# Order of scores, bias, and input parts in a fused attention and layer norm kernel

## The chip, the core and the metric

The kernel runs on one core of a Trainium2 chip. The metric is the time of one launch on the device, in microseconds (us), the median of several runs. The core has a matmul engine (PE, with its weight loads shown as PEld), three engines for elementwise work, DVE, ACT and GpSimd (POOL in the profile), and SP, which here issues the DMAs. The engines run side by side and wait for one another on semaphores. Matmul results land in PSUM, everything else lies in SBUF.

## What is computed

128 graphs of 128 nodes with 384 features, 12 heads of 32:

```python
q = (x @ Wq.T).reshape(B, N, 12, 32)
k = (x @ Wk.T).reshape(B, N, 12, 32)
v = (x @ Wv.T + bv).reshape(B, N, 12, 32)
a = einsum('bnhd,bmhd->bhnm', q, k) * SCALE + adj[:, None]
pad_mask = all(a == 0, axis=-1)
a = nan_to_num(softmax(where(pad_mask[..., None], -inf, a)))
o = einsum('bhnm,bmhd->bnhd', a, v).reshape(B, N, 384)
out = layernorm(x + o @ Wo.T + bo)
```

## The kernel before

The kernel works on graphs one by one, and on inputs by quads of four graphs; there are 32 quads. In a quad q the four stretches are called G0 to G3 here, one per graph. Every engine has its own program, written by hand in a fixed order, and `over_quads` unrolls it; each program runs ahead or behind by a fixed number of graphs.

For accuracy, the operands of the projections are split in two parts, `hi` and `lo`, and `split_product` (L208) adds three products in one PSUM bank. ACT makes `xT_hi` from `xT_raw` (`keep_xT_hi`, L375), DVE subtracts to make `xT_lo` (`keep_xT_lo`, L484), in three parts of 128 features per quad. `xT_raw` is a single buffer, loaded by SP (`load_xT`).

PE per stretch b, before: attention of graph b (`attend`, L252: twelve products, each on 32 columns of the array), the scores of graph b + 2 (`scores`, L229: twelve products, each on 32 rows of the array), six transposes of the probabilities of graph b + 1 (`transpose_probs`, L240), a projection of v or of q and k for a later graph or quad (L211 to L213), the output projection of graph b (`project_out`, L265), six more transposes, and one or two more projections. At the end of G2 stands `project_qk` of part 0 for the quad after next, which waits for all three parts of its `xT_lo` (`pe.wait_ge(xT_lo_done, CHUNKS * q + 3 * CHUNKS)`, L323).

DVE per stretch b (`graph`, L578): `keep_oT_lo` (after ACT's `oT_hi`), four bias trios for graph b + 2 (`bias_trio`, L504, adds the bias to three heads and finds the row maximum), in some stretches `keep_xT_lo` or `keep_v`, the first half of the mask (`mask_half`: `neg_sum`, `inv_sum`, `live`, `row_scale`), the residual (`y_sb`), `stats`, `mean_var`, `var_eps`, then `normalise` (`out_sb`), which waits for GpSimd's `inv_std`, and the second half of the mask.

ACT per stretch (L413): `oT_hi`, two copies of transposed probabilities to `pT` (L401), exponentials of graph b + 2 in trios, two more copies to `pT`, the last exponentials, with the copies `qkT` and `xT_hi` between them.

GpSimd per stretch (L664): `fold_half` twice, `scale_half` (multiplies the probabilities by `row_scale`), `inverse_std`, `add_bo` (adds the output bias to x of the next graph, in SBUF), `scale_half` for the other half.

Of the kernel before, what the change touches and what calls it, by code (L numbers as in the profile page):

```python
# [26 lines left out]
CHUNKS = HIDDEN // P  # L27
ROWS = P // HEAD
QUAD = 4
QUADS = BATCH // QUAD  # L30
# [15 lines left out]
def attention_kernel(nc, x, xT, adj, wq_t, wk_t, wv_t, wo_t, bv, bo, out):  # L46
# [7 lines left out]
    with ctx:  # L54
# [100 lines left out]
        def _(sp):  # L155
# [27 lines left out]
            load_x(QUAD, 1)  # L183

            def quad(j, p, has_next, has_after):
                q = 2 * j + p

                if has_after:
                    sp.wait_ge(xT_lo_done, CHUNKS * q + 2 * CHUNKS)
                    load_xT(q + 2)  # L190
                for b in range(QUAD):
                    sp.wait_ge(out_done, QUAD * q + b + 1)
                    sp.dma_start(out[bass.ds(QUAD * q + b, 1), :, :].rearrange("b n f -> n (b f)"),
                                 out_sb[:, b, :]).then_inc(out_stored[b], 16)
                    if b == 1 and has_after:
                        sp.wait_ge(neg_a_done, 16 * q + 16)
                        load_adj(QUAD * q + 2 * QUAD, p)
                if has_after:
                    load_x(QUAD * q + 2 * QUAD, p)
# [7 lines left out]
        def _(pe):  # L207
# [65 lines left out]
            def quad(j, p, has_next, has_after):  # L273
                q = 2 * j + p
                nxt, aft = ahead(j, p, 1), ahead(j, p, 2)

                pe.wait_ge(y_read, QUAD * q + 1)
                attend(j, p, 0)
                pe.wait_ge(neg_a_done, 16 * q + 8)
                scores(j, p, 2)  # L280
# [9 lines left out]
                if has_next:  # L290
                    pe.wait_ge(y_read, QUAD * q + 2)
                    project_qk(*nxt, 3, 0)
                pe.wait_ge(v_done, QUAD * q + 4)
                attend(j, p, 1)
                pe.wait_ge(neg_a_done, 16 * q + 12)
                scores(j, p, 3)
# [11 lines left out]
                attend(j, p, 2)  # L308
                if has_next:
                    pe.wait_ge(qk_done, QK * q + 2 * QK)  # L310
                    pe.wait_ge(neg_a_done, 16 * q + 16)
                    scores(*nxt, 0)
                transpose_probs(j, p, 3, 0)
# [12 lines left out]
                if has_next:  # L326
                    pe.wait_ge(v_done, QUAD * q + QUAD + 2)
                attend(j, p, 3)
                if has_next:
                    pe.wait_ge(neg_a_done, 16 * q + 20)  # L330
                    scores(*nxt, 1)
                    transpose_probs(*nxt, 0, 0)
# [41 lines left out]
        def _(act):  # L374
# [38 lines left out]
            def graph(j, p, b, has_next, has_after):  # L413
# [19 lines left out]
                if b == 2 and has_after:  # L433
                    keep_xT_hi(*aft, 2)
# [7 lines left out]
                if b == 0 and has_after:  # L442
                    act.wait_ge(v_psum, QUAD * (2 * j + p) + QUAD)
                    keep_xT_hi(*aft, 0)
                if b == 1 and has_next:
                    keep_qk(*nxt, 5, turn)
                if b == 3 and has_after:
                    keep_qk(*aft, 2, turn)
                if b == 1 and has_after:
                    keep_xT_hi(*aft, 1)  # L450
# [32 lines left out]
        def _(dve):  # L483
# [94 lines left out]
            def graph(j, p, b, has_next, has_after):  # L578
                nxt, aft = ahead(j, p, 1), ahead(j, p, 2)
                turn = 1 - ATTEND_BANK[b]  # L580
                more2 = b + 2 < QUAD or has_next
                keep_oT_lo(j, p, b)
                if more2:
                    for trio in range(4):
                        bias_trio(*later(j, p, b, 2), trio)
# [9 lines left out]
                statistics(j, p, b)  # L595
                mean_variance(j, p, b)
                add_eps(j, p, b)
                if b == 2 and has_after:
                    keep_xT_lo(*aft, 1)
                    keep_xT_lo(*aft, 2)  # L600
# [34 lines left out]
        def _(pool):  # L635
# [28 lines left out]
            def graph(j, p, b, has_next):  # L664
                more2 = b + 2 < QUAD or has_next
                if more2:
                    fold_half(*later(j, p, b, 2), 0)
                    fold_half(*later(j, p, b, 2), 1)
                    scale_half(*later(j, p, b, 2), 0)
                inverse_std(j, p, b)  # L670
                if b + 1 < QUAD or has_next:
                    add_bo(*later(j, p, b, 1))
# [53 lines left out]
```

## Time and profile before

| | |
|---|---|
| median of 3 runs | 1276.09 us (1274.07 to 1276.71) |
| profiled execution | 1274.01 us, span 1272.2 us |
| busy: PE, PEld | 1225.0 us (96%), 1053.9 us (83%) |
| busy: DVE, ACT, POOL | 1039.1 us (82%), 1022.4 us (80%), 859.3 us (68%) |
| granted clock of PE | 0.995 of full speed |
| DMA | 70 GB/s on average |

Busy shares are of the span. A busy PE isn't PE at its peak, since matmuls overlap. The quads repeat: each takes 38.87 us. So one of them, from 619.78 us to 658.65 us, is read below in order of time. A timeline row gives the start in us from the start of the span, the duration in us, the engine, the line, the operation, what it writes and what it reads, how many were merged, and in brackets the idle time ahead of it and who ended that.

### The profile page before, as it was taken

The page shows a single profiled execution, that of the slowest core. Times are in us where ns is not written, and L with a number is a line of the kernel's source. Part 1 is how long each engine was busy: PE and PEld are TensorE (multiplying, and loading weights), DVE is VectorE, ACT ScalarE, POOL GpSimd, SP SyncE. Part 2 cuts the span into 40 slices and gives each one's busy share as a digit, 9 for nine tenths or more (in the row PEclk, how much of TensorE's full clock was granted, in tenths as well). Part 3 has the DMA queues.
Part 4 walks back from the last instruction along what each step waited for, and adds up shares of the span by engine and source line. Part 5 has one row for each costly group of instructions (what it writes and reads, how often), then busy time and mean ns, then how long its engine had stood idle before and what let it go on. Part 6 is the DMA issues. An engine that isn't in the chain of part 4 may idle for free.

```text
span 1272.2 us, 34265 instructions
## 1 busy us (share of the span) xinstructions
PE 1225.0 (96%) x11742; PEld 1053.9 (83%) x11742; DVE 1039.1 (82%) x5094; ACT 1022.4 (80%) x4007; POOL 859.3 (68%) x775
## 2 busy tenths in 40 slices
PE   8999999999999999999999999999999999999986
PEld 7888888888888888888888888888888888888875
DVE  5778888888888788888888887888888888878886
ACT  6877888878788778888887887788887878877874
POOL 1766767667667667676676676676766766766675
PEclk9999999999999999999999999999999999999998
DMA  6022112222122221122221222211222202222100
GB/s 228 22 70 84 61 46 84 78 70 78 34 79 78 70 84 59 47 84 78 70 78 34 79 78 70 84 63 43 84 78 70 78 32 80 79 70 84 47 26 32
DMA packets 58895, 88.85 MB, mean 70 GB/s; under 512 B 3680, under 2 KB 54624, under 8 KB 58720
## 3 DMA queue, kind: packets, MB, share of 16 engines
q1 hardware_dynamic: 58720, 86.65, 20.2%
q8 instruction: 93, 1.52, 0.5%
q14 instruction: 82, 0.67, 0.2%
HBM read 61.47 MB, written 25.17 MB: 68 GB/s over the span
## 4 chain that ended last, share of the span: by engine, by line
PE 70%; DVE 24%; issue 3%; POOL 2%; ACT 1%; DMA 0%; DVEq 0%; POOLq 0%; SPq 0%
PE turn_bank L211 16%; PE turn_bank L213 16%; PE turn_bank L212 16%; PE pT_bank L248 9%; PE score_bank L235 7%; PE turn_bank L260 6%; DVE neg_a L511 6%; DVE out_sb L575 3%; DVE xT_lo L487 3%; DVE stats L560 3%; DVE y_sb L555 3%; DVE neg_sum L523 2%; POOL inv_std L661 1%; DVE v_sb L501 1%; DVE mean_var L564 1%
## 5 line engine op out<-in xcount | busy, mean ns | idle before, releaser
L396 ACT ACTIVATE probs<-neg_a,neg_max 128x128 f32<-128x128 f32 x1536 | 596.6, 398 | 1.9 <-DVE neg_max L511 1.9
L654 POOL TENSOR_TENSOR probs<-probs,row_scale 128x768 f32<-128x768 f32 x256 | 376.6, 1471 | 191.7 <-DVE row_scale L539 191.7
L647 POOL TENSOR_TENSOR fold<-neg_a 128x384 f32<-128x384 f32 x256 | 271.8, 1062 | 168.6 <-DVE neg_max L511 168.6
L511 DVE CUSTOM_DVE_ANT_0 neg_a<-score_bank,adj_sb 128x128 f32<-128x128 f32 x1536 | 333.2, 285 | 0.2
L403 ACT ACTIVATE pT<-pT_bank 128x384 f32<-128x384 f32 x512 | 220.8, 485 | 103.4 <-PE pT_bank L248 103.3
L396 ACT ACTIVATION_READ_ACCUMULATOR probs<-neg_a,neg_max 128x1 f32 x1536 | 302.8, 197 | 0.0
L211 PE MATMUL turn_bank<-xT_hi,w_hi 128*128 128x512 f32 x576 | 241.0, 418 | 29.4 <-DVE xT_lo L487 27.6
L213 PE MATMUL turn_bank<-xT_hi,w_lo 128*128 128x512 f32 x576 | 227.7, 395 | 0.0
L212 PE MATMUL turn_bank<-xT_lo,w_hi 128*128 128x512 f32 x576 | 227.6, 395 | 0.0
L248 PE MATMUL pT_bank<-ident,probs 128*128 128x128 f32 x1536 | 217.3, 278 | 0.3 <-ACT pT L403 0.3
L389 ACT ACTIVATE qkT<-turn_bank 128x512 f32<-128x512 f32 x192 | 113.7, 592 | 100.2 <-PE turn_bank L213 96.8
L248 PEld LDWEIGHTS pT_bank<-ident,probs 128*128 128x128 f32 x1536 | 173.9, 141 | 20.9 <-issue 1.2
L575 DVE TENSOR_SCALAR out_sb<-y_sb,mean_var,inv_std 128x384 f32<-128x384 f32 x128 | 124.1, 969 | 43.3 <-POOL inv_std L661 43.3
L211 PEld LDWEIGHTS turn_bank<-xT_hi,w_hi 128*128 128x128 f32 x576 | 108.5, 188 | 57.3 <-DVE xT_lo L487 39.2
L548 DVE TENSOR_TENSOR oT_lo<-turn_bank,oT_hi 128x384 fp32r<-128x384 f32 x128 | 71.1, 555 | 93.2 <-ACT oT_hi L409 93.2
L640 POOL TENSOR_TENSOR x_sb<-x_sb,bo_sb 128x384 f32<-128x384 f32 x128 | 131.9, 1030 | 19.5 <-DMA x_sb<-x_dram 19.5
L523 DVE TENSOR_REDUCE neg_sum<-fold 128x6 f32<-128x384 f32 x256 | 138.8, 542 | 2.6 <-POOL fold L647 2.6
L211 PE MATMUL turn_bank<-w_hi,xT_hi 128*128 128x384 f32 x384 | 140.0, 365 | 0.0
L211 PE MATMUL turn_bank<-w_hi,oT_hi 128*128 128x384 f32 x384 | 130.0, 339 | 1.9 <-DVE oT_lo L548 1.7
L213 PE MATMUL turn_bank<-w_hi,oT_lo 128*128 128x384 f32 x384 | 129.9, 338 | 0.0
L212 PE MATMUL turn_bank<-w_lo,oT_hi 128*128 128x384 f32 x384 | 129.8, 338 | 0.0
L213 PEld LDWEIGHTS turn_bank<-xT_hi,w_lo 128*128 128x128 f32 x576 | 108.1, 188 | 26.1
(38 smaller groups left out, 2021.9 us busy)
## 6 DMA issues: line engine op xcount, KB each, us to landing
xT_raw<-xT_dram SPq DMA_DIRECT2D x32, 768.0 KB, 6.3
x_sb<-x_dram SPq DMA_DIRECT2D x32, 768.0 KB, 5.2
out_dram<-out_sb SPq DMA_DIRECT2D x128, 192.0 KB, 1.9
adj_sb<-adj_dram SPq DMA_DIRECT2D x32, 256.0 KB, 3.0
w_raw<-wq_t_dram SPq DMA_DIRECT2D x1, 576.0 KB, 5.7
w_raw<-wk_t_dram SPq DMA_DIRECT2D x1, 576.0 KB, 6.8
w_raw<-wv_t_dram SPq DMA_DIRECT2D x1, 576.0 KB, 7.8
w_raw<-wo_t_dram SPq DMA_DIRECT2D x1, 576.0 KB, 8.4
```

The lines of the kernel that those rows point to most:

```text
L211: nc.tensor.matmul(dst, stat_hi(c), mov_hi(c), start=(c == 0), stop=False)
L212: nc.tensor.matmul(dst, stat_hi(c), mov_lo(c), start=False, stop=False)
L213: last = nc.tensor.matmul(dst, stat_lo(c), mov_hi(c), start=False, stop=(c == CHUNKS - 1))
L248: last = nc.tensor.transpose(pT_bank[r][:, c * N:(c + 1) * N], probs[b % 2][:, 3 * trio + c, :], ident[:, :])
L396: last = nc.scalar.activation(probs[b % 2][:, u, :], neg_a[b % 2][:, u, :], ACT.Exp, bias=neg_max[b % 2][:, u:u + 1], scale=-1.0, accum_ou ...
L403: nc.scalar.activation(pT[:, CHUNKS * trio:CHUNKS * (trio + 1), :], pT_bank[trio % 2][:, 0:HIDDEN].rearrange("p (c n) -> p c n", c=CHUNKS) ...
L511: last = nc.vector.tensor_tensor_reduce(out=neg_a[b % 2][:, u, :], in0=score_bank[trio][:, c * N:(c + 1) * N], in1=adj_sb[p][:, b, :], sca ...
L523: nc.vector.tensor_reduce(neg_sum[:, u], fold[:, u, :], AX.X, ALU.add).then_inc(mask_steps, 1)
L575: nc.vector.tensor_scalar(out_sb[:, b, :], y_sb[:, :], mean_var[:, 0:1], inv_std[:, 0:1], ALU.subtract, ALU.mult).then_inc(out_done, 1)
L640: nc.gpsimd.tensor_tensor(x_sb[p][:, b, :], x_sb[p][:, b, :], bo_sb[:, :], ALU.add)\
L647: nc.gpsimd.tensor_tensor(fold[:, u, :], neg_a[b % 2][:, u, 0:N // 2], neg_a[b % 2][:, u, N // 2:N], ALU.add).then_inc(fold_done, 1)
L654: nc.gpsimd.tensor_tensor(probs[b % 2][:, u, :], probs[b % 2][:, u, :], row_scale[:, u].unsqueeze(2).broadcast_to([P, HALF, N]), ALU.mult) ...
```

## The change

No operation is added or taken away. On PE, the scores go ahead of the attention in G0, G1 and G3, and behind the first transposes in G2. On DVE, the first bias trio goes ahead of `keep_oT_lo` in G0, G1 and G3; part 1 of `xT_lo` moves from G2 to G1, and part 2 stands ahead of `mean_variance` in G2. On ACT, `xT_hi` parts 0 and 1 are made in G0, part 2 in G1. On GpSimd, `add_bo` goes ahead of the first `scale_half`. On SP, `xT_raw` is loaded three quads ahead, in G3, and no longer two quads ahead at the start of the quad.

```diff
@@ sync
+            sp.wait_ge(xT_lo_done, 2 * CHUNKS)
+            load_xT(2)
...
-                if has_after:
-                    sp.wait_ge(xT_lo_done, CHUNKS * q + 2 * CHUNKS)
-                    load_xT(q + 2)
                 for b in range(QUAD):
+                    if b == 3 and q + 3 < QUADS:
+                        sp.wait_ge(xT_lo_done, CHUNKS * q + 3 * CHUNKS)
+                        load_xT(q + 3)
@@ tensor
+                pe.wait_ge(neg_a_done, 16 * q + 8)
+                scores(j, p, 2)
                 pe.wait_ge(y_read, QUAD * q + 1)
                 attend(j, p, 0)
-                pe.wait_ge(neg_a_done, 16 * q + 8)
-                scores(j, p, 2)
...
+                pe.wait_ge(neg_a_done, 16 * q + 12)
+                scores(j, p, 3)
                 pe.wait_ge(v_done, QUAD * q + 4)
                 attend(j, p, 1)
-                pe.wait_ge(neg_a_done, 16 * q + 12)
-                scores(j, p, 3)
...
                 attend(j, p, 2)
+                transpose_probs(j, p, 3, 0)
                 if has_next:
                     pe.wait_ge(qk_done, QK * q + 2 * QK)
                     pe.wait_ge(neg_a_done, 16 * q + 16)
                     scores(*nxt, 0)
-                transpose_probs(j, p, 3, 0)
...
                 if has_next:
+                    pe.wait_ge(neg_a_done, 16 * q + 20)
+                    scores(*nxt, 1)
                     pe.wait_ge(v_done, QUAD * q + QUAD + 2)
                 attend(j, p, 3)
                 if has_next:
-                    pe.wait_ge(neg_a_done, 16 * q + 20)
-                    scores(*nxt, 1)
@@ scalar
-                if b == 2 and has_after:
+                if b == 1 and has_after:
                     keep_xT_hi(*aft, 2)
...
                     keep_xT_hi(*aft, 0)
+                    keep_xT_hi(*aft, 1)
...
-                if b == 1 and has_after:
-                    keep_xT_hi(*aft, 1)
@@ vector
+                if b != 2 and more2:
+                    bias_trio(*later(j, p, b, 2), 0)
                 keep_oT_lo(j, p, b)
                 if more2:
-                    for trio in range(4):
+                    for trio in range(0 if b == 2 else 1, 4):
                         bias_trio(*later(j, p, b, 2), trio)
...
                 statistics(j, p, b)
+                if b == 2 and has_after:
+                    keep_xT_lo(*aft, 2)
                 mean_variance(j, p, b)
                 add_eps(j, p, b)
-                if b == 2 and has_after:
+                if b == 1 and has_after:
                     keep_xT_lo(*aft, 1)
-                    keep_xT_lo(*aft, 2)
@@ gpsimd
                     fold_half(*later(j, p, b, 2), 1)
+                if b + 1 < QUAD or has_next:
+                    add_bo(*later(j, p, b, 1))
+                if more2:
                     scale_half(*later(j, p, b, 2), 0)
                 inverse_std(j, p, b)
-                if b + 1 < QUAD or has_next:
-                    add_bo(*later(j, p, b, 1))
                 if more2:
                     scale_half(*later(j, p, b, 2), 1)
```

Three places in the order of instructions. The lines of the changed kernel stand two to four further down. First, PE at the start of G2: the attention of graph 2 (the row that writes `turn_bank` from `pT`), the scores of the next quad's graph 0, the transposes of graph 3, and the first projection of v. Before:

```order
L260 MATMUL turn_bank<-pT,v_sb 32x128 x12
L235 MATMUL score_bank<-qkT 128x128 x12
L248 MATMUL pT_bank<-ident,probs 128x128 x6
L211 MATMUL turn_bank<-w_hi,xT_hi 128x384
L212 MATMUL turn_bank<-w_lo,xT_hi 128x384
```

Changed:

```order
L262 MATMUL turn_bank<-pT,v_sb 32x128 x12
L250 MATMUL pT_bank<-ident,probs 128x128 x6
L237 MATMUL score_bank<-qkT 128x128 x12
L213 MATMUL turn_bank<-w_hi,xT_hi 128x384
L214 MATMUL turn_bank<-w_lo,xT_hi 128x384
```

The scores now stand behind the six transposes.

Second, DVE in G2, from behind the bias and `v_sb`: the mask's first half, the residual, the statistics and the parts of `xT_lo`. Before:

```order
L523 TENSOR_REDUCE neg_sum<-fold 128x6
L528 RECIPROCAL inv_sum<-row_sum 128x6
L533 TENSOR_TENSOR live<-neg_max,neg_sum 128x6
L539 TENSOR_TENSOR row_scale<-live,inv_sum 128x6
L555 TENSOR_TENSOR y_sb<-turn_bank,x_sb 128x384
L560 BN_STATS stats<-y_sb 128x6
L564 BN_AGGR mean_var<-stats 128x2
L568 TENSOR_SCALAR var_eps<-mean_var 128x1
L487 TENSOR_TENSOR xT_lo<-xT_raw,xT_hi 128x512 x2
L501 TENSOR_TENSOR v_sb<-turn_bank,bv_sb 128x384
```

Changed:

```order
L524 TENSOR_REDUCE neg_sum<-fold 128x6
L529 RECIPROCAL inv_sum<-row_sum 128x6
L534 TENSOR_TENSOR live<-neg_max,neg_sum 128x6
L540 TENSOR_TENSOR row_scale<-live,inv_sum 128x6
L556 TENSOR_TENSOR y_sb<-turn_bank,x_sb 128x384
L561 BN_STATS stats<-y_sb 128x6
L488 TENSOR_TENSOR xT_lo<-xT_raw,xT_hi 128x512
L565 BN_AGGR mean_var<-stats 128x2
L569 TENSOR_SCALAR var_eps<-mean_var 128x1
L502 TENSOR_TENSOR v_sb<-turn_bank,bv_sb 128x384
```

One part of `xT_lo` is left in G2, and it stands two places earlier.

Third, GpSimd in any stretch of the steady part, from the two folds on. Before:

```order
L647 TENSOR_TENSOR fold<-neg_a 128x384 x2
L654 TENSOR_TENSOR probs<-probs,row_scale 128x768
L661 TENSOR_TENSOR inv_std<-var_eps,minus_half 128x1
L640 TENSOR_TENSOR x_sb<-x_sb,bo_sb 128x384
L654 TENSOR_TENSOR probs<-probs,row_scale 128x768
```

Changed:

```order
L651 TENSOR_TENSOR fold<-neg_a 128x384 x2
L644 TENSOR_TENSOR x_sb<-x_sb,bo_sb 128x384
L658 TENSOR_TENSOR probs<-probs,row_scale 128x768
L665 TENSOR_TENSOR inv_std<-var_eps,minus_half 128x1
L658 TENSOR_TENSOR probs<-probs,row_scale 128x768
```

`add_bo` (the row that writes `x_sb`) moved from behind `inv_std` to behind the folds.

## Rows read from the trace of the kernel before

**Rows 1.** Waits of PE: for whom, us in total, times, longest

```profile
PE turn_bank L211 <- DVE xT_lo L487: 27.6, 30, 1.1
PE turn_bank L260 <- ACT pT L403: 6.9, 4, 2.7
```

**Rows 2.** Timeline of PE, one steady quad: start, duration, line

```profile
627.35 0.34 PE L213 MATMUL turn_bank<-w_hi,xT_lo 128*128 128x384 f32 x1
...
629.39 0.40 PE L213 MATMUL turn_bank<-xT_hi,w_lo 128*128 128x512 f32 x1
629.72 0.86 PE L260 MATMUL turn_bank<-pT,v_sb 128*32 128x128 f32 x24
...
638.66 0.86 PE L260 MATMUL turn_bank<-pT,v_sb 128*32 128x128 f32 x24
639.45 0.95 PE L235 MATMUL score_bank<-qkT 32*128 32x128 f32 x24
640.33 0.88 PE L248 MATMUL pT_bank<-ident,probs 128*128 128x128 f32 x6
640.96 0.42 PE L211 MATMUL turn_bank<-w_hi,xT_hi 128*128 128x384 f32 x1
...
647.47 0.50 PE L211 MATMUL turn_bank<-xT_hi,w_hi 128*128 128x512 f32 x1 [0.91 <-DVE xT_lo L487]
```

**Rows 3.** Timeline of DVE, the same quad, and its last `out_sb`

```profile
627.72 0.56 DVE L501 TENSOR_TENSOR v_sb<-turn_bank,bv_sb 128x384 f32<-128x384 f32 x1 [0.49 <-PE turn_bank L213]
...
634.17 0.69 DVE L487 TENSOR_TENSOR xT_lo<-xT_raw,xT_hi 128x512 fp32r<-128x512 f32 x1
...
635.36 0.40 DVE L533 TENSOR_TENSOR live<-neg_max,neg_sum 128x6 f32<-128x6 f32 x1
...
638.29 1.15 DVE L575 TENSOR_SCALAR out_sb<-y_sb,mean_var,inv_std 128x384 f32<-128x384 f32 x1 [0.67 <-POOL inv_std L661]
...
640.29 0.56 DVE L548 TENSOR_TENSOR oT_lo<-turn_bank,oT_hi 128x384 fp32r<-128x384 f32 x1
640.77 0.28 DVE L511 CUSTOM_DVE_ANT_0 neg_a<-score_bank,adj_sb 128x128 f32<-128x128 f32 x1
...
643.30 0.55 DVE L501 TENSOR_TENSOR v_sb<-turn_bank,bv_sb 128x384 f32<-128x384 f32 x1
...
644.35 0.17 DVE L533 TENSOR_TENSOR live<-neg_max,neg_sum 128x6 f32<-128x6 f32 x1
644.55 0.17 DVE L539 TENSOR_TENSOR row_scale<-live,inv_sum 128x6 f32<-128x6 f32 x1
644.63 0.55 DVE L555 TENSOR_TENSOR y_sb<-turn_bank,x_sb 128x384 f32<-128x384 f32 x1
645.22 0.56 DVE L560 BATCH_NORM_STATS2 stats<-y_sb 128x6 f32<-128x384 f32 x1
...
646.10 1.31 DVE L487 TENSOR_TENSOR xT_lo<-xT_raw,xT_hi 128x512 fp32r<-128x512 f32 x2
...
1269.35 0.48 DVE L575 TENSOR_SCALAR out_sb<-y_sb,mean_var,inv_std 128x384 f32<-128x384 f32 x1 [0.66 <-POOL inv_std L661]
```

**Rows 4.** Timeline of GpSimd (POOL), the same quad

```profile
634.34 1.40 POOL L647 TENSOR_TENSOR fold<-neg_a 128x384 f32<-128x384 f32 x1 [0.25 <-DVE neg_max L511]
...
638.22 1.00 POOL L640 TENSOR_TENSOR x_sb<-x_sb,bo_sb 128x384 f32<-128x384 f32 x1
...
643.46 1.03 POOL L647 TENSOR_TENSOR fold<-neg_a 128x384 f32<-128x384 f32 x1 [0.25 <-DVE neg_max L511]
644.79 1.47 POOL L654 TENSOR_TENSOR probs<-probs,row_scale 128x768 f32<-128x768 f32 x1 [0.30 <-DVE row_scale L539]
646.26 0.95 POOL L661 TENSOR_TENSOR inv_std<-var_eps,minus_half 128x1 f32<-128x1 f32 x1
```

**Rows 5.** Timeline of ACT, the `pT` pair ahead of attention 2

```profile
636.68 0.86 ACT L403 ACTIVATE pT<-pT_bank 128x384 f32<-128x384 f32 x2
```

## The prediction

> **What bounds the kernel now.** I read the waits first, then one steady quad in order of time, engine by engine. The waits of the matmul engine [rows 1] show it almost never idle: 27.6 us before L211, released by DVE's `xT_lo` (L487), 30 times, and 6.9 us in 4 waits for `pT`, which lie at the first and the last graphs. In the steady quad from 619.78 to 658.65 us the only stop of PE is the one at 647.47 [rows 2]: `project_qk` of the quad after next needs all three `xT_lo` parts, and DVE ends the last two at 646.10 + 1.31 = 647.41 [rows 3]; PE goes 0.06 later. Call the four stretches of a quad G0 to G3, each from one attention to the next: attention 1 stands at 629.72 (A1), attention 2 at 638.66 (A2) [rows 2]. That projection starts 8.81 after A2 (647.47 - 638.66). So PE's length is settled in G2 by a chain on DVE: first bias 640.77, last bias ends 643.30, `y_sb` 644.63, `stats` 645.22, `xT_lo` pair 646.10 [rows 3].
>
> **How DVE and GpSimd meet.** This decides the case. `live` (L533), a DVE operation with two SBUF inputs, takes 0.17 at 644.35. At 635.36 it takes 0.40: it ends at 635.76, 0.02 after the `fold` that GpSimd runs from 634.34 to 635.74 [rows 3, 4]. That `fold` is itself stretched to 1.40 from the 1.03 of the one at 643.46: it began 0.17 after an `xT_lo` on DVE that ends at 634.86 [rows 3, 4], and from there runs 0.88, so 0.15 of its start-up was done while it stood. `out_sb` (L575) takes 1.15 at 638.29, beside `add_bo` (638.22, 1.00), and 0.48 at 1269.35 with GpSimd idle [rows 3, 4]. And `inv_std` at 646.26, where the `xT_lo` pair was already queued, takes 0.95, ending well behind the first of them. So of the two, the one that comes second stands until the first has ended. The Trainium skill, "SBUF — State Buffer", section "Who interferes with whom", has the same rule: a DVE instruction with two SBUF inputs contends with a GpSimd instruction that reads SBUF, and whichever issues first keeps the pair while the other fully blocks. The rows agree (0.40, 1.15, 1.40); it speaks against this change.
>
> **The change, part by part.**
> (1) Scores ahead of attention in G0, G1, G3. PE does the same work. Each switch between full-array, row-tiled and column-tiled matmuls leaves 0.33 between starts (629.39 to 629.72) where the spacing is 0.23, so 0.10 a switch [rows 2]. Before: projection, attention, scores, transposes, three switches; now three too. I take 0; the new pairs may cost or return 0.05 each, so up to 0.15 in three stretches, 4 us either way in all. In G2 the order is now attention, transposes, scores, projection. Transposes run from 640.33 to the projection at 640.96, 0.63, and there was no switch behind them [rows 2]; now there is one ahead of the scores and one behind: scores start at A2 + 0.79 + 0.80 = 1.59, and PE's own work up to the projection grows by 0.2. If PE set the end that were 6 us over 30 quads; beside the chain below it is hidden. The Trainium skill, "TensorEngine Tiling (Array Packing)", section "Key Properties", says that changing the tiling mode drains TensorE; the 0.33 agrees, and by that rule alone the change costs those 6 us.
> (2) One trio of the bias (three of 0.21, 0.63) ahead of `oT_lo` in G0, G1, G3. DVE waits there for `oT_hi` anyway, and the scores now come 0.88 earlier (the length of scores, 639.45 to 640.33 [rows 2]). So in G1 the last bias ends 0.63 earlier: it ended at 634.17, A1 + 4.45 [rows 3]; now A1 + 3.82. `oT_lo` isn't later.
> (3) The copies `xT_hi` on ACT. Part 2 moves from G2 into G1, ahead of `pT` for attention 2. The pair of `pT` starts at 636.68, A1 + 6.96, and takes 0.86 [rows 5]. Now transposes come 0.88 earlier after A1 and the copy (no longer than the 0.69 of its DVE twin) is added: end about 7.63, while A2 comes at 8.94 - 0.88 = 8.06. Hidden, 0.4 to spare; were the cover gone it would cost at most 0.3 a quad. Part 1 goes behind `exp` of G0, where nothing waits for it. The load of `xT` is issued a graph before the old place: SP is past its wait for `out_done` there, and the stores and the `adj` and `x` loads keep their order. Nothing.
> (4) `xT_lo` part 1 goes to G1, behind `var_eps`; part 2 stands alone in G2, ahead of `mean_var`. By DVE's own times that is the gain: from first bias to `y_sb` 3.86, to `stats` 0.59, then 0.48 (as from `oT_lo` 640.29 to the bias 640.77) to `xT_lo`, 0.69, 0.06 to PE [rows 3].
> (5) `add_bo` now stands between the second `fold` and the first `scale`. Before, GpSimd was idle there, and after `inv_std` it ran beside `out_sb`. Now `add_bo` starts as `fold` ends. `row_scale` has two SBUF inputs and comes after that: in G2 `fold` ends at 643.46 + 1.03 = 644.49, `row_scale` starts 644.55 [rows 3, 4]. It stands for the whole of `add_bo`, and with it all that is queued on DVE (`y_sb`, `stats`, `xT_lo`, `out_sb`). In return `out_sb` runs beside an idle GpSimd, 0.48 instead of 1.15.
>
> **The walk.** G1, from the last bias E1 = A1 + 3.82: `xT_lo` part 0 starts, `fold` ends E1 + 1.57 (as 635.74 - 634.17), `add_bo` + 2.57, `row_scale` ends + 2.59, `y_sb` starts 0.09 before that (644.72, 644.63), + 2.50. `xT_lo` part 1 is issued 1.47 later (646.10 - 644.63), + 3.97. `scale` starts 0.07 after `row_scale` ends, + 2.66, and takes 1.47, + 4.13; `xT_lo` ends 0.55 after that, `inv_std` + 5.08. From `out_sb` to the next `oT_lo` it was 2.00 (638.29 to 640.29); less 0.67, 1.33: `oT_lo` at + 6.43, which is A1 + 10.25 = A2 + 2.19. It was A2 + 1.63. First bias 0.48 later, A2 + 2.67 [rows 3, 4]. The scores would allow 2.57: last column group 0.67 after the start at 1.59, and 0.31 until DVE sees it (L501 came 0.37 after the start of the last matmul at 627.35, of which 0.06 is its greater width [rows 2, 3]).
> G2: last bias ends 2.67 + 2.53 = 5.20; `fold` 5.36 to 6.39; `row_scale` would come at 2.67 + 3.78 = 6.45, 0.06 too late; `add_bo` until 7.39, `row_scale` ends 7.41, `y_sb` 7.32, `stats` 7.91, `xT_lo` issued 8.39. `scale` runs from 7.48 to 8.95, so `xT_lo` ends at 9.50 and PE goes at 9.56, against 8.81: 0.75 longer. G0 and G3 lose time on DVE as well. From a last bias: `fold` ends 1.19, `add_bo` 2.19, `scale` 2.3 to 3.75, `inv_std` at most 0.67 more (the wait at 638.29), 4.4, next bias trio 1.33 later, 5.75, then 0.63, `oT_lo` 0.48, nine biases 1.90: 8.8 for a round. Those stretches last 8.9 to 9.9 without a wait, so PE isn't held there; the margin in the short one is 0.1. PE itself would be ready at 7.94.
> 30 quads x 0.75 = +22.5 us. Ends: the scores now fill part of the waits for `pT` at the start and the end, about 0.9 in each of four: -3.5. 1274.0 + 19.0 = 1293.0; the median of the runs is 2.1 above the profiled one, so 1295.
>
> **Rivals.**
> A, faster: GpSimd and DVE don't hold each other up in the new places (`scale` has been seen ahead of `xT_lo` only with its last 0.16, at 646.10). Then bias at 2.57, `y_sb` 6.43, `stats` 7.02, `xT_lo` 7.50 to 8.19, PE 8.25: 0.56 less a quad, 16.8, with the ends 20.3: 1256. It decides whether `xT_lo` of G2 gets in ahead of `scale`: unheld it comes at 7.50, while `scale` behind `add_bo` comes at 7.3, a margin of 0.2. For it: that margin is small. Against: the 0.40 of `live`, an operation of the same kind, in the same place.
> B, halfway: `row_scale` is held and `scale` doesn't hold `xT_lo`: 8.39 + 0.69 + 0.06 = 9.14, + 0.33, so +9.9 - 3.5: 1282.5.
> C, the gain of (4) and the loss of (5) cancel, for instance if `add_bo` slips behind `row_scale` and `xT_lo` is held for half of `scale`: 8.8, no change but the ends, about 1273.
> If only `scale` holds, and not `add_bo`, the end is 7.39 + 1.47 + 0.55 + 0.06 = 9.47, and the forecast stands.
>
> **How the numbers follow.** Forecast 0.64, A 0.17, B 0.14, C 0.05. Unknowns of the forecast: switches of PE 4 us either way, the ends 2, the walk 0.1 a quad, 3. The likeliest case alone reaches from 1288 to 1301. The range goes down over B and C to 1267 and leaves A out. Within 0.2% is about what a measurement of this kernel can't tell from none. Faster 0.19, same 0.04, slower 0.77.
>
> **What would show it.** In the profile after: `row_scale` (L539 before) near 1.0 instead of 0.17 where `add_bo` runs; `out_sb` near 0.5 on average; `xT_lo` of G2 well over 0.69, ending with `scale` + 0.55; PE's wait for `xT_lo` still there, 30 times, about 1.6 each; the quad 39.6 instead of 38.87. Wrong, if `row_scale` stays at 0.17 and that wait shrinks to about 0.3: then A.

## The result and the profile after

The changed kernel takes 1297.6 us (median of 4 runs, 1297.0 to 1298.2), the kernel before 1275.1 (median of 4 runs beside it, 1274.1 to 1276.7): a ratio of 1.0175, 95% interval 1.0158 to 1.0193. It is slower by 1.75%, as forecast (1295.0, range 1267 to 1301). The profiled execution took 1297.29 us, its span 1295.5, the granted clock 0.996 of full speed.

The waits of PE, total, times and longest, in the kernel after. The first row answers to [rows 1], where it was 27.6 us:

```profile
PE turn_bank L213 <- DVE xT_lo L488: 43.4, 30, 1.5
PE turn_bank L213 <- DVE oT_lo L549: 5.3, 6, 1.2
PE turn_bank L262 <- DVE y_sb L556: 3.0, 2, 1.9
```

The three groups of DVE instructions in the kernel after: count, busy us, mean ns of one, idle time ahead:

```profile
L540 DVE TENSOR_TENSOR row_scale<-live,inv_sum 128x6 f32<-128x6 f32 x256 | 138.3, 540 | 8.7
...
L488 DVE TENSOR_TENSOR xT_lo<-xT_raw,xT_hi 128x512 fp32r<-128x512 f32 x96 | 79.6, 831 | 11.2 <-ACT xT_hi L380 11.2
...
L576 DVE TENSOR_SCALAR out_sb<-y_sb,mean_var,inv_std 128x384 f32<-128x384 f32 x128 | 61.4, 480 | 49.0 <-POOL inv_std L665 49.0
```

`out_sb` is down to 480 ns on average, from 969, `row_scale` up from 0.17 us [rows 3] to 0.54 on average (0.92 to 0.94 in 126 of 256, 0.17 in the rest), and `xT_lo` to 0.83 from 0.69. Now one steady quad. PE from the attention of graph 1 (A1, 642.07) over that of graph 2 (A2, 650.13) to the wait, which answers to [rows 2]:

```profile
641.19 0.95 PE L237 MATMUL score_bank<-qkT 32*128 32x128 f32 x24
642.07 0.86 PE L262 MATMUL turn_bank<-pT,v_sb 128*32 128x128 f32 x24
...
650.13 0.86 PE L262 MATMUL turn_bank<-pT,v_sb 128*32 128x128 f32 x24
650.92 0.88 PE L250 MATMUL pT_bank<-ident,probs 128*128 128x128 f32 x6
651.73 0.95 PE L237 MATMUL score_bank<-qkT 32*128 32x128 f32 x24
...
659.66 0.50 PE L213 MATMUL turn_bank<-xT_hi,w_hi 128*128 128x512 f32 x1 [1.44 <-DVE xT_lo L488]
```

DVE in G2 of that quad, as [rows 3]:

```profile
652.25 0.55 DVE L549 TENSOR_TENSOR oT_lo<-turn_bank,oT_hi 128x384 fp32r<-128x384 f32 x1
652.81 0.29 DVE L512 CUSTOM_DVE_ANT_0 neg_a<-score_bank,adj_sb 128x128 f32<-128x128 f32 x1
...
656.59 0.92 DVE L540 TENSOR_TENSOR row_scale<-live,inv_sum 128x6 f32<-128x6 f32 x1
657.43 0.55 DVE L556 TENSOR_TENSOR y_sb<-turn_bank,x_sb 128x384 f32<-128x384 f32 x1
...
658.49 1.12 DVE L488 TENSOR_TENSOR xT_lo<-xT_raw,xT_hi 128x512 fp32r<-128x512 f32 x1
```

GpSimd beside it, as [rows 4]:

```profile
655.51 1.02 POOL L651 TENSOR_TENSOR fold<-neg_a 128x384 f32<-128x384 f32 x1 [0.25 <-DVE neg_max L512]
656.47 1.01 POOL L644 TENSOR_TENSOR x_sb<-x_sb,bo_sb 128x384 f32<-128x384 f32 x1
657.59 1.47 POOL L658 TENSOR_TENSOR probs<-probs,row_scale 128x768 f32<-128x768 f32 x1
```

`add_bo` ends at 657.48, `row_scale` at 657.51. `scale` ends at 659.06, `xT_lo` at 659.61, PE goes at 659.66, 9.53 after A2. The quad takes 39.60 us instead of 38.87: G0 9.93, G1 8.06, G2 12.70, G3 8.90, before 9.94, 8.94, 11.10 and 8.89. The 0.88 that leaves G1 is the block of scores, which now runs once more in G2; what G2 grows beyond that is the 0.73 a quad.

### The profile page after: what moved, and what is told of

Its sections match the earlier page's. It is cut to its first block, busy times and chain, and to the rows that moved or that the text cites. A ratio compares the mean times of both kernels' runs of the same rounds, so it can differ in the third digit from the quotient of the medians.

```text
span 1295.5 us, 34265 instructions
## 1 busy us (share of the span) xinstructions
PE 1232.0 (95%) x11742; PEld 1054.0 (81%) x11742; DVE 1094.3 (84%) x5094; ACT 1018.4 (79%) x4007; POOL 855.3 (66%) x775
## 4 chain that ended last, share of the span: by engine, by line
PE 79%; DVE 17%; issue 3%; POOL 1%; ACT 0%; DMA 0%; POOLq 0%; SPq 0%; DVEq 0%
PE turn_bank L213 17%; PE turn_bank L214 17%; PE turn_bank L215 17%; PE pT_bank L250 12%; PE score_bank L237 9%; PE turn_bank L262 7%; DVE neg_a L512 7%; DVE xT_lo L488 3%; DVE neg_sum L524 1%; DVE y_sb L556 1%; DVE stats L561 1%; DVE v_sb L502 1%; POOL probs L658 0%; DVE row_scale L540 0%; DVE live L534 0%
## 5 line engine op out<-in xcount | busy, mean ns | idle before, releaser
L512 DVE CUSTOM_DVE_ANT_0 neg_a<-score_bank,adj_sb 128x128 f32<-128x128 f32 x1536 | 341.0, 287 | 48.8 <-PE score_bank L237 48.5
L213 PE MATMUL turn_bank<-xT_hi,w_hi 128*128 128x512 f32 x576 | 241.3, 419 | 45.1 <-DVE xT_lo L488 43.4
L411 ACT ACTIVATE oT_hi<-turn_bank 128x384 fp32r<-128x384 f32 x128 | 63.3, 495 | 105.7 <-PE turn_bank L262 105.7
L540 DVE TENSOR_TENSOR row_scale<-live,inv_sum 128x6 f32<-128x6 f32 x256 | 138.3, 540 | 8.7
L644 POOL TENSOR_TENSOR x_sb<-x_sb,bo_sb 128x384 f32<-128x384 f32 x128 | 129.3, 1010 | 19.8 <-DMA x_sb<-x_dram 19.8
L237 PEld LDWEIGHTS score_bank<-qkT 32*128 32x128 f32 x3072 | 97.2, 186 | 40.7 <-issue 39.4
```

The source lines that it names most:

```text
L213: nc.tensor.matmul(dst, stat_hi(c), mov_hi(c), start=(c == 0), stop=False)
L237: last = nc.tensor.matmul(score_bank[r][:, c * N:(c + 1) * N], qkT[p][row, c, tok], qkT[p][row, CHUNKS + c, tok], start=True, stop=True)
L512: last = nc.vector.tensor_tensor_reduce(out=neg_a[b % 2][:, u, :], in0=score_bank[trio][:, c * N:(c + 1) * N], in1=adj_sb[p][:, b, :], sca ...
L540: nc.vector.tensor_tensor(row_scale[:, u], live[:, u], inv_sum[:, u], ALU.mult)\
```

## The experiments

Every time stands against the kernel before on the same chip, 1274.4 to 1274.8 us. A quad is from one attention 0 to the next. Quads, G2 lengths and waits are of the profiled execution; a quad is the length that most of the steady ones have.

**e1: everything but `add_bo`.**

```diff
+                if more2:
+                    scale_half(*later(j, p, b, 2), 0)
+                inverse_std(j, p, b)
                 if b + 1 < QUAD or has_next:
                     add_bo(*later(j, p, b, 1))
-                if more2:
-                    scale_half(*later(j, p, b, 2), 0)
-                inverse_std(j, p, b)
```

> The changed kernel, with add_bo back behind inv_std on GpSimd and nothing else undone. Theory (DVE and GpSimd hold each other up in SBUF, the second stands until the first has ended): row_scale is back at 0.17 us on average, out_sb near 0.97 again. In G2 y_sb starts 3.86 after the first bias and xT_lo 1.07 after that, but scale starts 4.0 after the first bias and so is still ahead of xT_lo (4.9 after): xT_lo stays held until scale + 0.55. First bias at about A2 + 2.7 (out_sb takes 1.15 again beside add_bo in G1), so PE goes 2.7 + 4.0 + 1.47 + 0.55 + 0.06 = 8.8 after attention 2, as in the kernel before (8.81). Less the ends, 3.5: about 1272 us. Rival 1 (only row_scale's hold mattered, xT_lo isn't held by scale): 8.4, 1259 us. Rival 2 (the loss comes from the scores behind the transposes in G2, GpSimd's order is harmless): stays at about 1297 us.

Measured: 1274.02 us, ratio 0.9996 (0.9987 to 1.0006), quad 38.85. DVE in G2 of e1, then GpSimd, then PE:

```profile
684.93 1.11 DVE L488 TENSOR_TENSOR xT_lo<-xT_raw,xT_hi 128x512 fp32r<-128x512 f32 x1
```

```profile
684.03 1.47 POOL L658 TENSOR_TENSOR probs<-probs,row_scale 128x768 f32<-128x768 f32 x1 [0.31 <-DVE row_scale L540]
```

```profile
686.10 0.50 PE L213 MATMUL turn_bank<-xT_hi,w_hi 128*128 128x512 f32 x1 [0.69 <-DVE xT_lo L488]
```

Without `add_bo` in front, `scale` still starts 0.90 ahead of `xT_lo`, and `xT_lo` ends 0.54 after `scale` does (685.50, 686.04). So `scale` holds `xT_lo` in its new place whether or not `add_bo` stands in front.

**e2: `add_bo` alone**, in the kernel before (the edit of GpSimd's order in the change, nothing else).

```diff
+                if b + 1 < QUAD or has_next:
+                    add_bo(*later(j, p, b, 1))
+                if more2:
                     scale_half(*later(j, p, b, 2), 0)
                 inverse_std(j, p, b)
-                if b + 1 < QUAD or has_next:
-                    add_bo(*later(j, p, b, 1))
```

> The kernel before with add_bo ahead of the first scale on GpSimd, that edit alone. Theory: row_scale is held behind add_bo in every graph (mean near 0.54 us, since the second half of the mask isn't), y_sb in G2 starts 0.8 later after the first bias, so does the pair of xT_lo; out_sb falls to 0.48 and gives 0.1 back by way of an earlier first bias. PE goes about 9.5 after attention 2 instead of 8.81: 30 x 0.7 = +21 us, about 1296 us. Rival (the swap costs nothing, or gains what out_sb gets shorter, and the loss is one of the other edits): 1270 to 1276 us.

Measured: 1299.64 us, ratio 1.0186 (1.0169 to 1.0203), quad 39.64. The wait and the group of `row_scale` in e2:

```profile
PE turn_bank L211 <- DVE xT_lo L487: 50.4, 30, 1.8
...
L539 DVE TENSOR_TENSOR row_scale<-live,inv_sum 128x6 f32<-128x6 f32 x256 | 134.9, 527 | 8.7
```

This one edit costs 25 us, somewhat more than the whole change. It is 3.6 us more than I expected. Some 2 us of that are in the steady quad, which grew by 0.77 and not by 0.70: the shorter `out_sb` didn't bring the first bias forward (A2 + 2.11, as before), and PE goes at A2 + 9.56. In the profiled run, the slowest of the four (1301.27), one quad took 41.28 besides: from 343.2 to 346.4 us, behind a stop of PE of 1.79, the granted clock was 0.69 of full speed, and products of 0.40 took 0.63. The place of the rest is not settled.

**e6: scores and bias trio alone**, in the kernel before (PE's four moves, of which the lines below show G0's and G2's, and the trio ahead of `keep_oT_lo`).

```diff
+                pe.wait_ge(neg_a_done, 16 * q + 8)
+                scores(j, p, 2)
                 pe.wait_ge(y_read, QUAD * q + 1)
                 attend(j, p, 0)
-                pe.wait_ge(neg_a_done, 16 * q + 8)
-                scores(j, p, 2)
...
                 attend(j, p, 2)
+                transpose_probs(j, p, 3, 0)
                 if has_next:
                     pe.wait_ge(qk_done, QK * q + 2 * QK)
                     pe.wait_ge(neg_a_done, 16 * q + 16)
                     scores(*nxt, 0)
-                transpose_probs(j, p, 3, 0)
...
+                if b != 2 and more2:
+                    bias_trio(*later(j, p, b, 2), 0)
                 keep_oT_lo(j, p, b)
                 if more2:
-                    for trio in range(4):
+                    for trio in range(0 if b == 2 else 1, 4):
```

> The kernel before with the changed order on PE (scores ahead of attention in G0, G1, G3, behind the transposes in G2) and the bias trio ahead of oT_lo in G0, G1, G3; xT parts, add_bo and loads as before. Theory: the first bias of G2 can start only at A2 + 2.57 (it was 2.11), y_sb 6.43, first of the pair xT_lo held by scale until about 8.1, pair ends about 9.2, PE at 9.3 against 8.81: +0.45 x 30 = +14, less 3.5 at the ends: about 1286 us. Rival (the order on PE is free or a gain, since it fills waits): 1272 us or less.

Measured: 1292.35 us, ratio 1.0133 (1.0117 to 1.0148), quad 39.45. The first bias of G2 stands at A2 + 2.67, with the scores at A2 + 1.60, PE goes at A2 + 9.38, and its wait is this:

```profile
PE turn_bank L211 <- DVE xT_lo L487: 39.5, 30, 1.6
```

The miss of 6 us has two parts: the bias comes 1.07 after the start of the scores where I had 0.98, some 3 us over 30 quads, and the ends give nothing back.

**e7: e6 with G2 in the old order.**

```diff
                 attend(j, p, 2)
-                transpose_probs(j, p, 3, 0)
                 if has_next:
                     ...
                     scores(*nxt, 0)
+                transpose_probs(j, p, 3, 0)
```

> e6 (scores ahead of attention in G0, G1, G3 and the bias trio ahead of oT_lo, everything else as before) but G2 in the old order, scores ahead of the transposes. Theory (the 0.58 a quad of e6 come from the scores behind the transposes in G2, which hold the first bias until A2 + 2.67): oT_lo at A2 + 1.64 as in e6, first bias 0.48 behind it, 2.12, so all behind it 0.55 earlier: G2 12.0, quad 38.90, 1292.4 - 16.5 = 1276 us. Rival (the order of G2 costs PE itself, or the loss comes from the other three stretches): G2 stays at 12.4 or more, 1288 or more.

Measured: 1274.82 us, ratio 1.0001 (0.9992 to 1.001), quad 38.92, G2 11.99, first bias at A2 + 2.11. The theory holds: the scores ahead of the attention in three stretches, with the trio, cost nothing on balance, and the order of G2 costs 17.5 us (1292.35 less 1274.82). Three waits of PE in e7:

```profile
PE turn_bank L211 <- DVE xT_lo L487: 27.6, 30, 1.0
PE turn_bank L211 <- DVE oT_lo L548: 8.2, 6, 2.2
PE turn_bank L260 <- ACT pT L403: 2.9, 3, 1.5
```

The waits for `pT` at the ends fell from 6.9 [rows 1] to 2.9, about the 3.5 us that the prediction took for the ends; but those for `oT_lo`, of which the kernel before has one of 1.7, came in their place.

**e8: what in `add_bo` holds DVE?** The change, with `add_bo` replaced by a memset about as long, of a tile that nothing reads. So e8 leaves out the output bias.

```diff
+        idle_sb = sb("idle_sb", [P, 1152])
...
-                nc.gpsimd.tensor_tensor(x_sb[p][:, b, :], x_sb[p][:, b, :], bo_sb[:, :], ALU.add)\
-                    .then_inc(xb_done, 1)
+                nc.gpsimd.memset(idle_sb[:, :], 0.0).then_inc(xb_done, 1)
```

> The changed kernel, in which GpSimd fills 1152 columns of an unused tile at the place of add_bo instead of adding bo to x. So the output bias is left out of the result. The fill reads nothing from SBUF and takes about as long (1.0 us, from 0.2 us for 128 columns in the first rows of GpSimd). Theory (a DVE operation with two SBUF inputs is held only by a GpSimd operation that reads SBUF): row_scale is back at 0.17 us, y_sb in G2 comes 3.9 after the first bias; scale still starts after the fill, 4.8 after the first bias, just ahead of xT_lo (4.9), which stays held: PE about 9.4 after attention 2, about 1293 us. Rival 1 (it is GpSimd being busy that holds DVE, or a dependence in the order, whatever it does): row_scale stays at 0.54 on average, 1297 us. Rival 2 (xT_lo gets in ahead of scale): 1256 us, with xT_lo at 0.69.

Measured: 1293.68 us, ratio 1.0145 (1.013 to 1.016), quad 39.53. DVE, then GpSimd, in G2 of e8:

```profile
694.33 0.17 DVE L541 TENSOR_TENSOR row_scale<-live,inv_sum 128x6 f32<-128x6 f32 x1
...
695.48 1.76 DVE L489 TENSOR_TENSOR xT_lo<-xT_raw,xT_hi 128x512 fp32r<-128x512 f32 x1
```

```profile
694.19 1.07 POOL L645 MEMSET idle_sb<- 128x1152 f32 x1
695.21 1.48 POOL L658 TENSOR_TENSOR probs<-probs,row_scale 128x768 f32<-128x768 f32 x1
```

A memset, which reads nothing, doesn't hold `row_scale`: it ran inside the memset in 0.17. The time is lost all the same: `scale` comes at the memset's end and holds `xT_lo` until 697.24. What counts in G2 is how far `scale` is delayed. After A2 it starts at 6.70 in e1, at 7.34 in e8 and at 7.46 in the change, and PE's projection at 8.78, 9.42 and 9.53: both later by 0.64 in e8, and by 0.76 and 0.75 in the change. So the held `row_scale` adds only the last 0.11, since `scale` waits for it too.

The Trainium skill, "SBUF — State Buffer", section "Who interferes with whom", states that a DVE instruction with two SBUF inputs contends with a GpSimd instruction that reads SBUF, and not with one that only writes it. e8 agrees: with a memset in the same slot `row_scale` stays at 166 ns on average.

**e4: the parts of `xT_lo` early**: e1 with parts 0 and 1 at the start of G1, ahead of the bias, and part 2 behind `var_eps` of G1.

```diff
+                if b == 1 and has_after:
+                    keep_xT_lo(*aft, 0)
+                    keep_xT_lo(*aft, 1)
                 if b != 2 and more2:
                     bias_trio(*later(j, p, b, 2), 0)
...
-                if b == 1 and has_after:
-                    keep_xT_lo(*aft, 0)
...
-                if b == 2 and has_after:
-                    keep_xT_lo(*aft, 2)
                 mean_variance(j, p, b)
                 add_eps(j, p, b)
                 if b == 1 and has_after:
-                    keep_xT_lo(*aft, 1)
+                    keep_xT_lo(*aft, 2)
```

> A version of my own: the changed kernel with add_bo back behind inv_std, xT_lo parts 0 and 1 at the very start of G1, where DVE waits for scores (from 0.1 to 1.0 after they start), and part 2 behind var_eps in G1; nothing of xT_lo in G2. Theory: PE's wait for xT_lo is gone, PE goes 7.94 after attention 2, its own pace (0.87 less than before, and 0.1 for a projection that starts without a stop): 30 x 0.97 = 29, ends 3.5: about 1243 us. Rival (another chain takes over at once, residual to y_read or v_sb): 1255 us or more, with a new wait of PE in G2.

Measured: 1248.74 us, ratio 0.9789 (0.9773 to 0.9806), quad 37.98, no wait of PE for `xT_lo`. The mean of `xT_lo` is 1090 ns, longer than the 831 of the change, and it costs next to nothing, since PE doesn't wait for it. It is 5.7 us above my 1243. PE's start in G2 was right, A2 + 7.93 for 7.94. About 2.4 us of the miss lie in the steady quad, 37.98 where 37.90 was expected; most of the rest lies at the ends, which give nothing back, with 8.6 us of waits for `oT_lo`. In all kernels here in which PE sets the pace a quad is 37.93 to 38.03.

**e5: e4 with `add_bo` ahead of `scale`**, as in the change.

```diff
+                if b + 1 < QUAD or has_next:
+                    add_bo(*later(j, p, b, 1))
                 if more2:
                     scale_half(*later(j, p, b, 2), 0)
                 inverse_std(j, p, b)
-                if b + 1 < QUAD or has_next:
-                    add_bo(*later(j, p, b, 1))
```

> The version with the xT_lo parts early (1248.7 us), but add_bo ahead of scale as in the change. It asks what the hold of row_scale costs where xT_lo isn't behind it. Theory: y_sb comes 0.9 later after the bias in G1 and G2, and the second half of the mask in G1 ends later too, so the first bias of G2 comes later than A2 + 3.1; y_read then comes later than the 7.94 at which PE wants turn_bank: a new wait of PE, for y_sb, 0.5 to 1.0 a quad: 1264 to 1280 us. Rival (the hold costs only by way of xT_lo): 1249 us.

Measured: 1269.59 us, ratio 0.9956 (0.9941 to 0.9971), quad 38.68. A wait of PE in e5:

```profile
PE turn_bank L213 <- DVE y_sb L556: 10.3, 31, 0.3
```

With `xT_lo` out of the way `add_bo` costs 0.70 a quad still: it holds `row_scale`, behind which `y_sb` is queued, and the bank that `y_sb` reads comes free late, so that PE starts the projection at A2 + 8.51 and not at 7.93. So the place of `add_bo` hurts by either of two chains.

**e10: e4 with all of `xT_hi` in G0 and G2 in the old order.**

```diff
-                transpose_probs(j, p, 3, 0)
                 if has_next:
                     ...
                     scores(*nxt, 0)
+                transpose_probs(j, p, 3, 0)
...
-                if b == 1 and has_after:
-                    keep_xT_hi(*aft, 2)
...
                     keep_xT_hi(*aft, 0)
                     keep_xT_hi(*aft, 1)
+                    keep_xT_hi(*aft, 2)
```

> A version of my own: parts early, add_bo behind inv_std, all three xT_hi in G0 on ACT, and in G2 the scores ahead of the transposes as before the change (attention, scores, transposes). Theory: one switch of the array and its 0.1 to 0.2 us less on PE in each quad: 37.8 instead of 38.0, about 1243 us. Rival (qkT part 5 isn't there yet when the scores of G2 are due, PE waits about 0.3, or oT_hi comes later behind the third copy): 1249 us or more.

Measured: 1247.89 us, ratio 0.9789 (0.9774 to 0.9803), quad 38.00. The switch is saved, but the gain isn't there: the rival's wait for `qkT` takes its place, 0.2 and not 0.3 a quad, and the time stays 1 us under the rival's 1249. The wait in e10:

```profile
PE score_bank L237 <- ACT qkT L391: 6.5, 31, 0.7
```

The scores of G2 start at A2 + 1.05 there, and not at 0.79. Behind the transposes they don't wait for `qkT`, and pay about the same for the switches.

**e11: one part in the gap.** e1 with part 2 of `xT_lo` between `live` and `row_scale` of G2, that is, ahead of the step that releases `scale`.

```diff
-                    mask_half(*later(j, p, b, 2), 0)
+                    for step in (mask_sum, mask_reciprocal, mask_live):
+                        step(*later(j, p, b, 2), 0)
+                    if b == 2 and has_after:
+                        keep_xT_lo(*aft, 2)
+                    mask_scale(*later(j, p, b, 2), 0)
...
-                if b == 2 and has_after:
-                    keep_xT_lo(*aft, 2)
```

> The changed kernel with add_bo back behind inv_std, and in G2 xT_lo part 2 between live and row_scale instead of behind stats. Scale can't have started there, since it waits for row_scale. Theory: xT_lo takes 0.69 instead of 1.12, ends 7.1 after attention 2, PE's wait for it goes to nothing although y_sb comes 0.6 later (y_read at about 7.8, PE wants 7.94): quad 38.0, about 1249 us, as the version with the parts early. Rival (DVE's whole length from attention to y_sb sets PE's end, the place of xT_lo in it doesn't matter): 1270 us or more.

Measured: 1247.15 us, ratio 0.9777 (0.9761 to 0.9794), quad 37.93. DVE, then GpSimd, in G2 of e11:

```profile
668.69 0.68 DVE L488 TENSOR_TENSOR xT_lo<-xT_raw,xT_hi 128x512 fp32r<-128x512 f32 x1
669.29 0.16 DVE L540 TENSOR_TENSOR row_scale<-live,inv_sum 128x6 f32<-128x6 f32 x1
```

```profile
667.72 1.02 POOL L653 TENSOR_TENSOR fold<-neg_a 128x384 f32<-128x384 f32 x1 [0.25 <-DVE neg_max L512]
669.53 1.47 POOL L660 TENSOR_TENSOR probs<-probs,row_scale 128x768 f32<-128x768 f32 x1 [0.79 <-DVE row_scale L540]
```

`xT_lo` takes 0.68 between the end of `fold` and the start of `scale`, which can't come earlier. The wait of PE for it is gone. This is the fastest kernel of the study, 27 us faster than before.

**e12: e11 with the old order of scores and bias**, on PE (G0 shown, G1 to G3 likewise) and DVE.

```diff
-                pe.wait_ge(neg_a_done, 16 * q + 8)
-                scores(j, p, 2)
                 pe.wait_ge(y_read, QUAD * q + 1)
                 attend(j, p, 0)
+                pe.wait_ge(neg_a_done, 16 * q + 8)
+                scores(j, p, 2)
...
-                if b != 2 and more2:
-                    bias_trio(*later(j, p, b, 2), 0)
                 keep_oT_lo(j, p, b)
                 if more2:
-                    for trio in range(0 if b == 2 else 1, 4):
+                    for trio in range(4):
```

> The same placement of the xT_lo and xT_hi parts as e11 (part 2 between live and row_scale in G2, add_bo behind inv_std), but PE's order and DVE's bias order as in the kernel before. Theory (the gain of e11 comes from the placement of the xT_lo parts alone, and the scores order only moves PE's time from G1 into G2): the kernel before without its 30 waits of 0.91 for xT_lo, 38.87 - 0.91 = 37.96 a quad, 1274.5 - 27.5 = 1247 us, no wait of PE for xT_lo, G2 about 10.2 and G1 8.94; ends as before (waits for pT about 7, for oT_lo about 2). Rival (the earlier scores are needed for it): quad over 38.3 with a wait of PE for xT_lo, oT_lo or y_sb in each quad, 1258 us or more.

Measured: 1248.55 us, ratio 0.9801 (0.9784 to 0.9817), quad 38.03, G2 10.23. The theory holds: nearly all of the gain of e11 is the place of the parts. With the old order the scores of G2 wait for `qkT`; the wait, and one row of it, 1.09 after an attention 2 at 664.08 (before the change the scores come 0.79 after it):

```profile
PE score_bank L237 <- ACT qkT L391: 7.4, 31, 0.7
...
665.17 0.95 PE L237 MATMUL score_bank<-qkT 32*128 32x128 f32 x24 [0.23 <-ACT qkT L391]
```

**e13: e11 with the bias trio back behind `oT_lo`** in G0, G1 and G3.

```diff
-                if b != 2 and more2:
-                    bias_trio(*later(j, p, b, 2), 0)
                 keep_oT_lo(j, p, b)
                 if more2:
-                    for trio in range(0 if b == 2 else 1, 4):
+                    for trio in range(4):
```

> e11 with the first bias trio back behind oT_lo in G0, G1, G3; the scores stay ahead of attention. Theory (at both ends of the program, where DVE comes late, the trio ahead of oT_lo makes the output projection wait: 8.5 us in 6 waits): those waits fall to about 2, waits for pT rise again by 1 to 4, the steady quad stays at 37.93, since the bias ends 0.63 later but xT_lo part 2 in G2 still ends by A2 + 7.7: 1244 us, between 1242 and 1248. Rival (the trio is needed in the steady part): a wait for xT_lo or v_sb of 0.2 or more in each quad, 1253 or more.

Measured: 1254.81 us, ratio 0.9843 (0.9829 to 0.9858), quad 38.23, 10 us over my expectation. At the ends it did what was expected: the six waits for `oT_lo`, 8.5 us in e11, became four of 3.9. But the steady quad grew by 0.30: the rival was right that the trio is needed there, and it acts through two chains that I hadn't put down. DVE, then PE, in G2 of e13:

```profile
674.54 0.55 DVE L556 TENSOR_TENSOR y_sb<-turn_bank,x_sb 128x384 f32<-128x384 f32 x1
```

```profile
675.24 0.47 PE L213 MATMUL turn_bank<-xT_hi,w_hi 128*128 128x512 f32 x1
```

`project_qk` of the quad after next needs `xT_lo` and also the bank that `y_sb` reads. `y_sb` ends at 675.09, PE goes 0.15 later, at A2 + 8.06; in e11 `y_sb` ends 0.35 earlier and PE goes at A2 + 7.92 without a stop. That is 0.14, and after this short stop the second product starts 0.31 behind the first instead of 0.24, another 0.07. The remaining 0.09 lies in G1. ACT, then PE, before attention 2 of the same quad:

```profile
666.20 0.84 ACT L405 ACTIVATE pT<-pT_bank 128x384 f32<-128x384 f32 x2
```

```profile
667.18 0.86 PE L262 MATMUL turn_bank<-pT,v_sb 128*32 128x128 f32 x24
```

The copies to `pT`, queued behind exponentials that need the later bias, end at 667.04, and attention 2 goes 0.14 later, at A1 + 8.15. In e11 they end 0.60 before attention 2, which goes at A1 + 8.06. The stops are too short for the view of the waits, which shows neither of them.

## Why the prediction was right, step by step

The runs make one path of single steps from the kernel before to the change: scores ahead in three stretches and the trio 0 (e7), the order of G2 +17.5 (e6 less e7), the placement of the input parts -18.3 (e1 less e6), `add_bo` +23.6 (the change less e1). That they add up to the whole, 22.8, is so by construction; the shares depend on the path. The same move of `add_bo` costs 25.0 in the kernel before (e2), 23.6 here and 20.9 in e4's place of the parts (e5).

**What bounds the kernel: right.** The chain on DVE that ends in `xT_lo` of G2 sets PE's length before and after; in all kernels where that chain is out of the way (e4, e10, e11, e12) the quad is 37.9 to 38.0.

**(1) PE's switches: right in mechanism and in size.** Scores in G2 start at A2 + 1.60 (1.59 forecast). e11 shows PE unhindered: its projection stands at A2 + 7.92, for which I had 7.94. The row is this, in e11:

```profile
670.27 0.40 PE L213 MATMUL turn_bank<-xT_hi,w_hi 128*128 128x512 f32 x1
```

The switches of G2 cost 0.20 a quad, as forecast: PE's stop ahead of the projection begins at A2 + 8.09 in the change (659.66 - 1.44) and at A2 + 7.90 in the kernel before (647.47 - 0.91). The quads of e11 and e12 agree, 37.93 against 38.03 less the 0.30 by which e12's scores come late.

**The first bias: right by luck.** The walk took the exit from G1 as its limit, `oT_lo` at 2.19 and the bias 0.48 behind it, 2.67, and put the scores' own limit at 2.57. Measured, `oT_lo` stands at 2.12, which would allow 2.60, and the bias comes at 2.68, 1.08 after the start of the scores; in e1, e6, e8 and e11, where `oT_lo` is earlier still (1.64 to 2.03), it stands at 2.67 or 2.68 too. So the scores set it in all of these. One error of 0.07 too late and one of 0.1 too early hid each other, and the hold in G1, which the walk let run on into G2, costs nothing there: `add_bo` acts in G2 alone.

**(2) The trio: right in the steady quad, wrong at the ends.** "`oT_lo` isn't later" fails there: e11 waits 8.5 us for it in 6 waits, e13 3.9 in 4, the kernel before 1.7. What it gives in the steady part of e11 is shown by e13, 0.30 a quad; in the change itself it was not tried alone.

**(3) `xT_hi` and the load: hidden, as said.** No wait of PE for `pT` or of DVE for `xT_hi` is new in the steady quad of e1 or of the change; DVE's idle time ahead of `xT_lo` is 11.2 us in all, in e6 with the old places 11.5. The `pT` pair ends at A1 + 7.47, for which I had 7.63, 0.59 before attention 2. How thin that cover is shows in e13, where it is gone.

**(4) The parts of `xT_lo`: right, and worth 18.3 us, but they give only what the order of G2 takes.** With the part alone in G2 it comes 0.90 behind the start of `scale`, and pays 0.43 for being second. e1 shows this without `add_bo`.

**(5) `add_bo`: right.** `row_scale` 0.92 in G2, held until 0.03 after `add_bo`; `out_sb` 0.48. Of the mechanism I had two holds in series. e8 shows that in G2 the second is enough: with the first one taken out the quad is still 39.53, and the first adds 0.08 a quad. `out_sb`, which the prediction counts among the rows for the hold, reads one tensor and two columns; its 1.15 beside `add_bo` and 0.48 without are measured, but no run shows which of its inputs makes it wait. The remark that the forecast stands "if only `scale` holds" was right, at 9.47 forecast against 9.42 for PE's start in e8 (697.29 less its A2, 687.87).

**The walk: 0.75 forecast, 0.73 measured.** Its points after A2, forecast and measured: first bias 2.67 and 2.68, `fold` 5.36 and 5.38, end of `add_bo` 7.39 and 7.35, `y_sb` 7.32 and 7.30, `scale` 7.48 and 7.46, `xT_lo` 8.39 and 8.36, its end 9.50 and 9.48, PE 9.56 and 9.53. 30 x 0.73 = 21.9. The wait for `xT_lo` was forecast at about 1.6 each and is 1.45 (43.4 in 30): I counted it from 7.94, where the projection could have started, and the profile counts it from the end of the product before, 8.09.

**The ends: the term that was mis-sized.** I had -3.5; the span grew by 23.3, of which 21.9 are the steady quads, so the ends cost +1.4. The waits for `pT` did shrink (from 6.9 to 0.7 in the change), but the first and last graphs now wait for `oT_lo` (5.3) and, with `add_bo` in front, for `y_sb` (3.0; e1 has no such wait). **The offset** between the median and the profiled run was 2.1 in the runs of before that I took it from, and 0.3 here. The one error is +4.9, the other -1.8 and the walk's -0.6, together 2.5, from 1295.1 to 1297.6. So the number is as close as it is partly because the offset made up for some of the ends.

**The rivals.** A (1256) needed `xT_lo` to come ahead of `scale` when nothing is held. e1 falsifies it: `row_scale` isn't held there, and `scale` is first by 0.90, a place that was to be seen from [rows 3, 4], where `scale` starts 0.07 after `row_scale` and `y_sb` and `stats` still stand ahead of `xT_lo`. The margin that I gave it, 7.50 against 7.3 for a `scale` behind `add_bo`, was already on the wrong side. B (1282.5) falls by the rows of the change, where `xT_lo` takes 1.12. C (1273) is what e1 shows for the change without `add_bo`, by another way: the parts and G2's order cancel.

## What to carry to other kernels

For a DVE operation with two SBUF inputs that someone waits for, look which GpSimd operation can start shortly before it, and put the DVE operation ahead of the instruction that releases that one, as e11 does. An idle gap of GpSimd was not free room here: what was moved into it held DVE itself, or, as the memset of e8, pushed the operation behind it onto the critical one of DVE. When several parts of a change touch one chain, run each one alone and each one left out; here +17.5, -18.3 and +23.6 hid in one number.

## What the runs showed that was not expected

A held operation with much to do ends about 0.55 after its holder, however long it stood: `xT_lo` of 128x512 takes 0.69 alone and ended 0.54 or 0.55 after `scale` in the change, in e1 and in e8, where it stood longest. So by these rows about 0.14 of it, an estimate, is done while it stands. `row_scale`, six elements wide, ended 0.03 after `add_bo`. The hold goes both ways in one pair: in e4 the first of two `xT_lo` held `scale`, which took 1.85, and `scale` then held the second. DVE, then GpSimd, in G1 of e4:

```profile
655.70 2.56 DVE L488 TENSOR_TENSOR xT_lo<-xT_raw,xT_hi 128x512 fp32r<-128x512 f32 x2
```

```profile
655.86 1.85 POOL L657 TENSOR_TENSOR probs<-probs,row_scale 128x768 f32<-128x768 f32 x1 [1.16 <-DVE row_scale L540]
```
